# RNN step with its high weights times both halves of the state in one 32-column matmul, the two column sets added on VectorE, the input projection in groups of 8 steps

## The reference

```python
# layer 0
h_next = jnp.tanh(h @ Wh + xw_t)                 # xw = x @ Wx + b
# layer 1
h_bar = xp_t + prev_h @ Wh                       # four gates, i f o g
next_c = f * prev_c + i * g
next_h = o * jnp.tanh(next_c)
# layer 2: two of four experts per batch entry (gelu(x @ w1 + b1) @ w2 + b2), and a shared expert of the same form
# layer 3: an adapter whose weights come from the condition
x = x + _L0(x, cond); x = x + _L1(x, cond); x = x + _L2(x, cond); x = x + _L3(x, cond)
```

## Time and profile before

| | |
|---|---|
| median of 3 runs | 1195.59 us (1194.09 to 1197.45) |
| the profiled execution: time, span | 1194.56 us, 1192.8 us |
| busy share PE, DVE, ACT, POOL | 96%, 74%, 43%, 34% |
| RNN of block 0 alone | 24 to 47 us |
| LSTM blocks 0 to 15 | 51 to 759 us |
| block 7 (matrix) from its first fc to the next block's | 371.10 to 416.51, 45.4 us |
| block 10 (no matrix work), the same | 505.38 to 548.47, 43.1 us |
| routed experts and adapter | to 1192.8 us |

### The profile page before, as it was taken

How to read it: one execution, slowest core, us unless ns; L and a number is a source line. 1 busy time by engine, 2 the same in 40 slices (tenths; PEclk the granted TensorE clock), 3 DMA queues, 4 the chain that set the end, 5 groups by cost and what they waited for, 6 DMA issues and landing times.

```text
span 1192.8 us, 58924 instructions
## 1 busy us (share of the span) xinstructions
PE 1144.3 (96%) x24138; PEld 1033.3 (87%) x24138; DVE 887.2 (74%) x3368; ACT 515.4 (43%) x1896; POOL 403.5 (34%) x1368
## 2 busy tenths in 40 slices
PE   5999999999999999999999999789999999999898
PEld 4889889889889889999999998678888888888677
DVE  6577888887887887787787778786666666666697
ACT  3344444444454444443444343323333333333476
POOL 2654454454454454454454440181000000000021
PEclk9658999999999999999999999899999999999899
DMA  8211202202112111110000000000000000000022
GB/s 242 73 40 43 78 4 79 78 5 79 48 36 79 32 51 27 15 15 11 4 4 5 4 4 4 2 1 2 2 2 2 2 1 2 2 2 2 4 75 85
DMA packets 43282, 37.17 MB, mean 31 GB/s; under 512 B 23128, under 2 KB 38794, under 8 KB 43020
## 3 DMA queue, kind: packets, MB, share of 16 engines
q1 hardware_dynamic: 42412, 33.12, 9.2%
q10 hardware_dynamic: 608, 0.30, 0.1%
HBM read 28.42 MB, written 4.98 MB: 28 GB/s over the span
## 4 chain that ended last, share of the span: by engine, by line
PE 86%; DVE 8%; ACT 2%; issue 2%; POOL 1%; DMA 1%; SPq 0%; DVEq 0%; POOLq 0%
PE bank L1087 17%; PE bank L1088 17%; PE bank L1089 17%; PE bank L1182 16%; PE bank L1188 8%; PE bank L1156 4%; DVE seq L742 2%; PE bank L1162 2%; PE bank L1238 1%; ACT tc L529 1%; DVE LH L789 1%; PE bank L1453 1%; PE bank L1228 1%; PE bank L1425 1%; DMA WE<-in_L_cond_b 1%
## 5 line engine op out<-in xcount | busy, mean ns | idle before, releaser
L1182 PE MATMUL bank<-LH,seq 128*128 128x16 f16 x8192 | 282.0, 170 | 12.4 <-DVE LH L789 11.0
L1182 PEld LDWEIGHTS bank<-LH,seq 128*128 128x128 f16 x8192 | 250.7, 96 | 43.9 <-DVE LH L789 32.2
L1087 PE MATMUL bank<-GH,WE 128*128 128x256 f16 x768 | 209.7, 273 | 6.6 <-DVE GH L771 6.3
L534 ACT ACTIVATE gel<-bank,seq 128x256 f32<-128x256 f32 x256 | 121.5, 475 | 217.3 <-PE bank L1089 217.1
L1087 PE MATMUL bank<-XHL,WE 128*128 128x256 f16 x768 | 210.2, 274 | 3.4 <-DVE XHL L752 3.2
L769 DVE CAST GH<-gel 128x256 f16<-128x256 f32 x384 | 122.1, 318 | 120.1 <-ACT gel L534 111.9
L1088 PE MATMUL bank<-XHL,WE 128*128 128x256 f16 x768 | 210.2, 274 | 0.0
L1089 PE MATMUL bank<-XHL,WE 128*128 128x256 f16 x768 | 210.2, 274 | 0.0
L1088 PE MATMUL bank<-GH,WE 128*128 128x256 f16 x768 | 209.5, 273 | 0.0
L1089 PE MATMUL bank<-GH,WE 128*128 128x256 f16 x768 | 209.5, 273 | 0.0
L518 ACT ACTIVATE tfig<-bank 128x96 f32<-128x96 f32 x256 | 64.2, 251 | 285.9 <-PE bank L1188 285.9
(11 more groups left out here) (184 smaller groups left out, 2599.5 us busy)
## 6 DMA issues: line engine op xcount, KB each, us to landing
stage<-in_L_cond_ew SPq DMA_DIRECT2D x8, 1024.0 KB, 8.7
stage<-in_L_cond_W SPq DMA_DIRECT2D x8, 1024.0 KB, 6.1
XHL<-in_x SPq DMA_DIRECT2D x8, 512.0 KB, 9.1
out<-WE SPq DMA_DIRECT2D x16, 256.0 KB, 2.2
stage<-in_L_cond_sw SPq DMA_DIRECT2D x2, 1024.0 KB, 5.3
scratch<-rows SPq DMA_DIRECT2D x96, 8.0 KB, 2.3
stage<-in_L_cond_Wx SPq DMA_DIRECT2D x1, 1024.0 KB, 9.0
stage<-in_L_cond_Wh SPq DMA_DIRECT2D x1, 1024.0 KB, 11.1
```

The lines of the kernel that those rows point to most:

```text
L534: nc.scalar.activation(gel[:, m % 2, :], banks[m % len(banks)][:, 0:256], ACT.Gelu_apprx_tanh, scale=scale, bias=bias).then_inc(s["a_g"], 1)
L1087: MM(out_, w(HI), x(HI), start=start, stop=False, skip_group_check=True)
L1182: MM(z, LW[:, h, 1, c, tile * P:(tile + 1) * P], LH[:, old, HI, c], start=False, stop=False, skip_group_check=True)
```

## The change

Each RNN step issues four matmuls of the LO weights (16 columns, after the HI state) and four of the HI weights by both halves of the state at once, 32 columns, after the LO state. RB now has two column sets for 8 steps instead of one for 16; the HI-by-LO products land in the second. DVE adds the two sets (`rnn_sum`) into rz in SBUF, between cell and hh of the LSTM step; ACT reads rz. `rnn_x` runs twice a block, 128 columns wide, at the head of RNN steps 0 and 8, after the sum of the step before. `split_x` moves to steps 9, 11 (casts) and 13, 14 (subtractions), in block 0 to 10 to 13, since XR is read until step 8. ACT's tanh of the cell comes ahead of the RNN's.

```diff
@@ rnn_step, ACT @@
-                z = RB[:, :].rearrange("p (m t b) -> p m t b", m=C, t=U)[:, :, r, :]
-                act.wait_ge(s["pe_r"], n + 1)
+                z = rz[:]
+                act.wait_ge(s["v_rz"], n + 1)
@@ block_steps, ACT @@
                     lstm_gates(it, u)
+                    lstm_cell(it, u)
                     if not last:
                         rnn_step(it + 1, u)
-                    lstm_cell(it, u)
@@ DVE @@
+            def rnn_sum(n):
+                pair = RB[:, :].rearrange("p (a m t b) -> p m t b a", a=2, m=C, t=G)[:, :, n % G]
+                dve.wait_ge(s["pe_r"], n + 1)
+                V.reduce_sum(rz[:], pair, AX_X).then_inc(s["v_rz"], 1)
...
                 V.tensor_scalar(cell[:], c2[:], 0.5, None, ALU.mult)
+                if rnn:
+                    rnn_sum(n + U)
                 dve.wait_ge(s["a_tc"], n + 1)
...
             for r in range(U):
+                rnn_sum(r)
...
-                if r == 1:
-                    dve.wait_ge(s["pe_rx"], 1)
-                if r in (1, 2, 3, 4):
-                    split_x(1, r - 1)
+                if r == 10:
+                    dve.wait_ge(s["pe_rx"], 2)
+                if r in (10, 11, 12, 13):
+                    split_x(1, r - 10)
...
-                    if xr and u in (4, 6, 8, 10):
-                        if u == 4:
-                            dve.wait_ge(s["pe_rx"], it + 2)
-                        split_x(it + 2, (u - 4) // 2)
+                    if xr and u in (9, 11, 13, 14):
+                        if u == 9:
+                            dve.wait_ge(s["pe_rx"], 2 * it + 4)
+                        split_x(it + 2, (9, 11, 13, 14).index(u))
@@ PE @@
-            def rnn_x(blk):
+            def rnn_x(blk, g):
                 pe.wait_ge(s["v_xr"], blk * 4 + 4)
+                if blk or g:
+                    pe.wait_ge(s["v_rz"], blk * U + g * G)
...
-                z = RB[:, :].rearrange("p (m t b) -> p m t b", m=C, t=U)
-                if not isinstance(n, int) or n > 0:
+                z = RB[:, :].rearrange("p (a m t b) -> p a m t b", a=2, m=C, t=G)
+                if r % G == 0 and n > 0:
+                    rnn_x(blk, r // G)
+                if n > 0:
                     pe.wait_ge(s["a_rh"], n)
                 for m in range(C):
                     for c in range(C):
-                        for h in (HI, LO):
-                            MM(z[:, m, r], RW[:, h, 1, c, m * P:(m + 1) * P], RH[:, old, HI, c],
-                               start=False, stop=False, skip_group_check=True)
+                        MM(z[:, 0, m, r % G], RW[:, LO, 1, c, m * P:(m + 1) * P], RH[:, old, HI, c],
+                           start=False, stop=False, skip_group_check=True)
...
-                        last = MM(z[:, m, r], RW[:, HI, 1, c, m * P:(m + 1) * P], RH[:, old, LO, c],
+                        last = MM(z[:, :, m, r % G], RW[:, HI, 1, c, m * P:(m + 1) * P], RH[:, old, :, c],
                                   start=False, stop=(c == C - 1), skip_group_check=True)
@@ block_steps, PE @@
-                if rx:
-                    pe.wait_ge(s["a_rh"], it * U + 2 * U)
-                    rnn_x(it + 2)
```

More of the change, by code:

```diff
@@ L95, in build_program @@
         rf = sb("rf", [P, 2, C, B], F32)
+        rz = sb("rz", [P, C, B], F32)
         x1s = sb("x1s", [P, 2, C, B], F32)
@@ L197, in build_program @@
             pe_cond v_cond a_cond v_gate pe_gate a_gate v_xr v_x2p v_sum
-            pe_rx pe_r a_rh  p_rlo p_x1 p_x1h p_x1l
+            pe_rx pe_r v_rz a_rh  p_rlo p_x1 p_x1h p_x1l
             pe_fig pe_o a_fig v_ig v_c2 a_tc v_hh v_h2 v_hl v_x2
@@ L772, in split_g, with lstm_step @@
                                 ).then_inc(s["v_gl"], 1)
-            def lstm_step(blk, u):
+            def rnn_sum(n):
+                pair = RB[:, :].rearrange("p (a m t b) -> p m t b a", a=2, m=C, t=G)[:, :, n % G]
+                dve.wait_ge(s["pe_r"], n + 1)
+                V.reduce_sum(rz[:], pair, AX_X).then_inc(s["v_rz"], 1)
+            def lstm_step(blk, u, rnn=True):
                 n = blk * U + u
@@ L892, in block_steps @@
                 for u in range(U):
-                    lstm_step(it, u)
+                    lstm_step(it, u, not last)
                     if last and u in extras:
@@ L1133, in _ @@
                 transpose_x(0, i)
-            def rnn_x(blk):
+            def rnn_x(blk, g):
                 pe.wait_ge(s["v_xr"], blk * 4 + 4)
+                if blk or g:
+                    pe.wait_ge(s["v_rz"], blk * U + g * G)
                 for m in range(C):
-                    z = RB[:, m * 256:(m + 1) * 256]
-                    MM(z, bias_pad[:, 4 * D + m * P:4 * D + (m + 1) * P], ones_pad[:, 0:256],
+                    z = RB[:, m * G * B:(m + 1) * G * B]
+                    MM(z, bias_pad[:, 4 * D + m * P:4 * D + (m + 1) * P], ones_pad[:, 0:G * B],
                        start=(m == 0), stop=False, skip_group_check=True)
@@ L1143, in rnn_x @@
                         last = three(z, lambda h: RW[:, h, 0, c, m * P:(m + 1) * P],
-                                     lambda h: XR[:, h, c].rearrange("p t b -> p (t b)"), False)
+                                     lambda h: XR[:, h, c, g * G:(g + 1) * G].rearrange("p t b -> p (t b)"), False)
                 last.then_inc(s["pe_rx"], 1)
@@ L1254, in _ @@
             pe.wait_ge(s["a_cond"], 2)
-            rnn_x(0)
+            rnn_x(0, 0)
             for r in range(U):
@@ L1266, in _ @@
                     fig_x(0, r - FIG_STEP)
-            pe.wait_ge(s["a_rh"], U)
-            rnn_x(1)
             pe.wait_ge(s["p_x1l"], U)
@@ L1306, in spread_logits, with block_steps @@
                    skip_group_check=True).then_inc(s["pe_gate"], 1)
-            def block_steps(it, first, last, rx, matrix=False):
+            def block_steps(it, first, last, matrix=False):
                 for u in range(U):
@@ L1341, in block_steps @@
                             low_rank(it - 1, LOW_WINDOWS.index(u), (it - 1) * M + (M + done))
-                if rx:
-                    pe.wait_ge(s["a_rh"], it * U + 2 * U)
-                    rnn_x(it + 2)
-            block_steps(0, True, False, True)
+            block_steps(0, True, False)
             pe.wait_ge(s["v_wlo"], SHARED_SPLIT)
             for it in range(1, 2 * E + 1):
[L1349 to L1353, removed]
+                block_steps(it, False, False, matrix=True)
+            for it in range(2 * E + 1, NB - 1):
+                block_steps(it, False, False)
+            block_steps(NB - 1, False, True)
             for j in range(M + 2):
```

## The result

The change takes 1220.47 us (median of 4 runs, 1219.07 to 1224.68) against 1195.3: a ratio of 1.0206, 95% interval 1.0175 to 1.0237. The profiled execution took 1219.07 us, span 1217.3, against 1192.8. The forecast was 1219. The total came out by errors that cancel, which the lengths of the blocks show. A step's length is the time from the start of its fc to that of the next one, a block's that of its 16 steps.

The account below looks back on a forecast made before the run. TensorE held 86% of the chain; odd LSTM steps were bound by the hh loop with DVE full. Matrix blocks +13.7, blocks 9 to 13 +3.2, block 14 +0.8, block 0 +1, prologue +5.7: +24.4 on 1194.6, 1219 us, range 1204 to 1238.

Parts of the forecast that it names:

- The moved splits, the largest term: Late split_x in odd steps without a DVE hole: a cast delays fc by 0.54 us, a subtraction costs 1.0.
- Step 14: Matrix blocks: 3.83 us before; the subtraction comes behind the weight piece and adds its 1.08 us.
- Step 0, "+0.15": First step of a matrix block: +0.15 us, extra PE work of half an rnn_x mostly under the late fc.
- a rival with a chance of 0.1: PE idles 2 us in steps 14 and 15, the clock falls, 1 to 2 us more per block: 1227 to 1235.
- The sum: DVE's rnn_sum, 0.20 to 0.25 us between cell copy and hh: cost 0, hh still at fc + 0.82.
- the rival: DVE starts nothing before the last operation ends; the sum adds 0.12 us in some 160 steps: 1238, chance 0.2.
- Fewer matmuls: 8 instead of 12 per RNN step, 25 ns each: PE-bound even steps gain 0.08 to 0.10 us, odd steps 0.
- ACT's order, "worth nothing": Cell tanh ahead of the RNN's in each step: no gain where hh already follows at its minimum.
- First 16 steps: RNN prologue before the first LSTM step: each step now waits in DVE's queue, +5.7 us net.
- Block 14: Block with both halves of rnn_x and no splits: +0.8 us.
- Blocks 9 to 13: Blocks with splits but no matrix work: +0.64 us each, +3.2 for the five.
- Block 1: Matrix block, +1.7 us like the others, plus some 2 us for a slower start after block 0's lost dense burst.

Follow-up runs that it names:

- the even places: Changed kernel, one buffer, splits at steps 8, 10, 12, 14, block 0 of the RNN as in the kernel before: 1186.62 us, ratio 0.993.
- the last variants: Changed kernel, RNN block 0 as before; splits at 8, 10, 12, 14: 1186.62 us; or at 4, 6, 8, 10 with a second XR buffer: 1195.63 us.

## Why the prediction was right, and where it was not

*The moved splits, the largest term*: right in mechanism, shown by the kernel with the moves alone and by the even places. For steps 8 to 15 of a matrix block I had +1.95 us, and +1.63 was measured. Sizes: a cast in an odd step 0.28 us (0.1 more in the next step), not 0.54, since fc starts under the cast; the subtraction of step 13 3.62 us for 3.89, that of step 14 4.72 for 4.91. Step 14 was priced as "a chain of add_bias, ACT's low_hi and the weight piece; the subtraction is behind it and adds its 1.08": so it is (+0.90), but 0.85 of it can be had by standing between addition and piece.

*Step 0, "+0.15"*: the step that failed. It measured +1.42 in blocks 2 to 8, by the clock, a rival with a chance of 0.1. That the total held in spite of it is luck. It covered what the late splits were overpriced by, and it is not all loss: PE then has no "issue" waits (steps 1 and 2: 5.48 us for 6.41), a net of 0.5 us a block. I had those waits before me in the kernel before and left them out.

*The sum*: right, by the run without it, as the trace of a 0.47 us operation followed after 0.39 had suggested. The rule of the Trainium skill (VectorE: DVE Perf Modes, The DRAIN you can't avoid), that the next operation waits for an empty pipe, has an exception in the same section, which the rival left out: "A next op that is not held starts earlier". The trace agrees with the exception: the sum starts 0.09 us behind the start of the cell copy of 0.18 us.

*Fewer matmuls*: I took 0.08 to 0.10 us in even steps. The price of a matmul (25 ns) was right, the gain was not the matmuls' own: alone they gain nothing in these steps, and the odd ones cost 0.09 more, by the rows of POOL and DVE because the two meet. Together with ACT's order and the sum they give it, which the calm steps of the last variants show (2.44 to 2.47 in odd and even steps alike).

*ACT's order, "worth nothing"*: true for hh in the kernel before (where the new order costs 0.6% by `rnn_x` and the "issue" waits), wrong for the changed one, where the old order costs 128 us.

*First 16 steps*: +5.4 for +5.7, by two errors that cancel. The sum costs 8.1 us there, and the rest of the change gives 2.7 back; I had 6.6, and 0.8 given back. *Block 14*: +0.83 for +0.8, right. *Blocks 9 to 13*: +0.35 for +0.64, by the casts. *Block 1*: +4.0, and +4.3 with block 0, where I had put 2.7 for both (the prediction's terms for block 0 and the start of block 1 add up to +1.3, not to the +1 it writes). Block 1's step 0 takes 5.16 us. The clock is 0.50 until 107 us, 4 us into block 1; in the kernel before it is 0.94 from 95 to 100 and 1.00 behind, and block 1 starts at 97.3. That is a longer stretch than the 2 us I allowed.

The range held; the total was hit because too little for blocks 0 to 8 (4.5 us), too much for blocks 9 to 13 (1.5) and the 2.5 us of the tail cancel.

## What to carry to other kernels

Price a moved operation in the step it goes to, not by its length: the same cast cost 0.28 us in an odd step and nothing in an even one (and up to 0.1 in the step behind either), and the same subtraction 0.8 in an odd step, 0.13 in an even one or, behind the operation that starts another engine's chain, 0. Before an operation is put into a wait, find out who starts what is waited for; if it is the waiting engine itself, its trigger must stay ahead. And a change that adds idle time to TensorE may pay it again in the clock: the idle stretch of 2.2 us cost 1.4 us more in the next step. What that is worth has to be measured: with the stretch filled, waits for instructions took 1.0 of the 1.4 back.

## What was unexpected

- Fewer matmuls made the kernel slower by 0.5%: two engines' small operations fell onto each other (a 32-element operation of DVE took 270 ns in the mean where POOL's began with it, 197 where they began just behind it).
- A stretch of 1.2 us without TensorE work was followed by the low clock in seven of eight blocks; one of 1.0 us, with 12 matmuls of zero weights ahead of it, in none. But one of 1.4 us, in the kernel before with the late splits, was followed by it in two of eight. So the length of the stretch alone does not decide, and no run here tells what else does.
- TensorE stalls of 0.34 to 2.5 us with no releaser come at most once per block, as 2 MB of loads end, and 1.2 to 1.6 us behind a late 16 KB packet of the queue that carries instructions; the two shown (2.52 and 1.54 us) were followed by a stretch at 1.2 GHz.
